# A DLRM tower on one core: gathers and gram by tiles of 128 samples, vecT held twice, an MLP block in front of each gram, ids 128 rows deep

## The reference

```python
e = jnp.stack([tbl_0[ids[:, 0]], ..., tbl_25[ids[:, 25]]], axis=1)
sd = jnp.einsum('bfd,bd->bf', e, dense)
ss = jnp.einsum('bfd,bgd->bfg', e, e)
pairs = ss[:, iu, ju]                      # triu, k=1
z = jnp.concatenate([dense, sd, pairs], axis=1)
h = jnp.concatenate([z, dense], axis=1)
h = jnp.maximum(h @ W_top1 + b_top1, 0.0)  # 512
h = jnp.maximum(h @ W_top2 + b_top2, 0.0)  # 256
y = h @ W_top3                             # 1
```

## Time and profile before

| | before |
|---|---|
| median of 3 runs | 405.81 us (405.66 to 406.05) |
| profiled execution, its own time | 407.06 us |
| span of the profiled execution, first to last instruction | 405.1 us |
| mean granted TensorE clock | 0.966 of full speed |
| PE busy | 360.1 us, 89% of the span |
| POOL busy | 261.0 us, 64% |
| DVE busy | 232.0 us, 57% |
| ACT busy | 185.9 us, 46% |

### The profile page before, as it was taken

How to read it: one execution, slowest core, us unless ns; L and a number is a source line. 1 busy time by engine, 2 the same in 40 slices (tenths; PEclk the granted TensorE clock), 3 DMA queues, 4 the chain that set the end, 5 groups by cost and what they waited for, 6 DMA issues and landing times.

```text
span 405.1 us, 13256 instructions
## 1 busy us (share of the span) xinstructions
PE 360.1 (89%) x6020; PEld 311.2 (77%) x6020; DVE 232.0 (57%) x326; ACT 185.9 (46%) x266; POOL 261.0 (64%) x279
## 2 busy tenths in 40 slices
PE   1965987968999989998999999998999899998895
PEld 0954976957888978897879878897879888897763
DVE  3999767862556825685557825684557835541300
ACT  2475523742137622674237623674147613673231
POOL 5777777777777777777777777777777777100000
PEclk9996698995999999999999999999999999999999
DMA  7867222222222222222222222222222222100000
GB/s 193 210 165 267 79 55 57 52 54 58 57 67 53 53 55 55 66 57 57 56 67 53 53 55 64 58 57 56 56 67 53 53 55 68 21 2 3 3 0 0
DMA packets 12271, 26.46 MB, mean 65 GB/s; under 512 B 5296, under 2 KB 6448, under 8 KB 12089
## 3 DMA queue, kind: packets, MB, share of 16 engines
q0 software_dynamic: 8704, 17.84, 17.7%
q1 hardware_dynamic: 3513, 7.79, 6.9%
HBM read 25.61 MB, written 0.01 MB: 63 GB/s over the span
## 4 chain that ended last, share of the span: by engine, by line
PE 77%; POOL 8%; issue 5%; ACT 4%; DMA 3%; DVE 2%; DVEq 0%; SPq 0%
PE sum_bank L421 31%; PE vec_bank L447 12%; PE work_bank L472 10%; POOL rows L224 8%; PE work_bank L482 7%; PE vec_bank L437 6%; PE work_bank L468 5%; PE id_bank L405 3%; DMA rows<-in_tbl,ids_all 2%; PE work_bank L490 2%; DVE onehot L260 1%; ACT late L350 1%; PE work_bank L460 1%; ACT vecT L325 1%; ACT vecT L318 1%
## 5 line engine op out<-in xcount | busy, mean ns | idle before, releaser
L224 POOL DMA_INDIRECT rows<-in_tbl,ids_all x272 | 260.2, 957 | 84.7 <-issue 79.6
L260 DVE TENSOR_TENSOR onehot<-id_bank,row_f 125x1024 fp32r<-125x1024 f32 x144 | 170.7, 1221 | 44.5 <-PE id_bank L405 27.9
L421 PE MATMUL sum_bank<-onehot,parts 125*128 125x256 f32 x1152 | 179.2, 303 | 6.5 <-DVE onehot L260 4.9
L421 PEld LDWEIGHTS sum_bank<-onehot,parts 125*128 125x128 f32 x1152 | 154.7, 200 | 19.7 <-issue 17.4
L325 ACT COPY vecT<-vec_bank 128x512 f32<-128x512 f32 (+1 forms) x72 | 86.3, 1199 | 13.4 <-PE vec_bank L437 13.4
L271 DVE STREAM_TRANSPOSE late<-late 128x832 f32<-128x832 f32 x16 | 28.8, 1798 | 95.8 <-ACT late L334 95.8
L318 ACT COPY vecT<-sum_bank 128x256 f32<-128x256 f32 x72 | 48.6, 678 | 45.1 <-PE sum_bank L421 44.9
L447 PE MATMUL vec_bank<-vecT 128*26 128x26 f32 x4096 | 53.0, 193 | 14.9 <-ACT vecT L325 9.7
L447 PEld LDWEIGHTS vec_bank<-vecT 128*26 128x26 f32 x4096 | 44.3, 104 | 25.9 <-ACT vecT L318 11.6
L437 PE MATMUL vec_bank<-ident,rows 128*128 128x128 f32 x272 | 44.5, 286 | 12.6 <-DMA rows<-in_tbl,ids_all 12.5
L334 ACT COPY late<-vec_bank 128x416 f32<-128x416 f32 x32 | 16.2, 505 | 77.7 <-PE vec_bank L447 75.4
(11 more groups left out here) (22 smaller groups left out, 73.5 us busy)
## 6 DMA issues: line engine op xcount, KB each, us to landing
rows<-in_tbl,ids_all POOLq DMA_INDIRECT x272, 2.5
late<-in_tbl SPq DMA_DIRECT2D x9, 480.0 KB
w_all<-in_weights SPq DMA_DIRECT2D x1, 1540.0 KB, 9.8
xT<-in_dense_t SPq DMA_DIRECT2D x8, 128.0 KB, 2.6
late<-in_weights SPq DMA_DIRECT2D x1, 256.0 KB, 2.7
ids_all<-in_ids SPq DMA_DIRECT2D x1, 208.0 KB, 2.5
late<-in_tbl SPq DMA_DIRECT2D x9, 20.0 KB
vecT<-in_ids_t SPq DMA_DIRECT2D x1, 72.0 KB
```

Of the source, the lines that this page charges most:

```text
L224: nc.gpsimd.indirect_dma_start(rows[:, j, n, t, :], None, tables[f], bass.IndirectOffsetOnAxis(ids_all[:, TD * d + t, f:f + 1], 0)).then_i ...
L260: nc.vector.tensor_tensor(onehot[:, use % RING, 0:width, :], bass.AP(got.tensor, got.offset, [got.ap[0], [0, width], [1, DS]]), bass.AP(nu ...
L421: last = nc.tensor.matmul(sum_bank[into % 2][:, 0:DS], parts[:, part, CH_AT[n] + c0 + c, :], onehot[:, use % RING, c, :], start=(p % PER = ...
```

## The change

What it does, part by part:

- The 17 gathered features go by tiles: the gathers of a tile (17) are issued before those of the next, `transpose_rows` takes four features of one tile (groups of 4, 4, 4, 4 and 1, so 5 groups for a tile), and their places in `vecT` follow in a row. There are still 272 gathers, and buffers for two tiles of them.
- `vecT` is held twice (one for each parity of the step), so that the next step's vectors can be written before this step's grams are done.
- Gram goes by tiles: two calls (h = 0, 1) for each tile, and the rest of the work on TensorE is cut in two halves, one for each tile: 9 packs of step d+1, the groups of the next tile, the pairs of this one.
- A unit of the MLP stands between a tile's last transposes and the next tile's first gram: `layer2(d-1, 0)` after tile 2d, `layer1(d, 0)` after tile 2d+1. The other units are spread behind the grams.
- `idsT` and `pick` are 128 rows deep, where they had 36 (the ids are filled up with rows of zeros); the ids' DMA brings 256 KB for 72 KB.
- The last step's MLP goes by tiles of 128 samples: that of tile 14 stands behind the grams of tile 15.
- `w1x` is summed on VectorE after the first `turn`, no longer at the end of the first step. `dots` is held once.
- The weights' rows are sorted on the host to the new places (`order`, `pair_row`); the amount of arithmetic is the same.

The core of the diff (left out: the same order written once more for ScalarE's drains, the counters, and the host's sorting):

```diff
-    FG = 2
+    FG = 4
...
-    ROWS_AT_FIRST = {1: 0, 3: 1, 5: 2, 7: 3, 9: 4, 11: 5, 13: 6, 15: 7, 17: 8}
-    ROWS_AFTER = {4: 1, 5: 2, 7: 3, 9: 4, 11: 5, 13: 6, 15: 7, 17: 8}
-    TURN_AFTER = {RING - 1: 0, RING + 1: 1}
-    PAIRS_AFTER = {6: 0, 10: 1}
-    X_AFTER = 8
+    ROWS_AT_FIRST = {3: 0, 6: 1, 9: 2, 12: 3, 15: 4}
+    ROWS_AFTER = {2: 0, 4: 1, 5: 2, 7: 3, 8: 4}
+    TURN_AFTER = RING + 1
+    LATE_LAYER1_AFTER = 3
+    PAIRS_AFTER = 6
+    X_AFTER = 7
...
-        vecT = sb("vecT", [P, DS, VECS])
+        vecT = sb("vecT", [P, 2, DS, VECS])
...
-        idsT = sb("idsT", [STEPS * NH // TWO, TWO * DS], fp32r)
+        idsT = sb("idsT", [P, TWO * DS], fp32r)
...
-        pick = sb("pick", [STEPS * NH // TWO, STEPS * NH // TWO], fp32r)
+        pick = sb("pick", [P, SPREADS], fp32r)
...
-            for d in range(STEPS):
+            for tile in range(TILES):
                 for j in range(GROUPS):
-                    if d:
-                        pool.wait_ge(vec_filled, rows_at(d - 1, j) + 1)
+                    if tile >= TD:
+                        pool.wait_ge(vec_filled, rows_at(tile - TD, j) + 1)
                     for n, f in enumerate(group(j)):
-                        for t in range(TD):
-                            nc.gpsimd.indirect_dma_start(
-                                rows[:, j, n, t, :], None, tables[f],
-                                bass.IndirectOffsetOnAxis(ids_all[:, TD * d + t, f:f + 1], 0)
-                            ).then_inc(gathered[j], 16)
+                        nc.gpsimd.indirect_dma_start(
+                            rows[:, tile % TD, FG * j + n, :], None, tables[f],
+                            bass.IndirectOffsetOnAxis(ids_all[:, tile, f:f + 1], 0)
+                        ).then_inc(gathered[tile % TD][j], 16)
...
+            for tile in range(TILES):
+                d, t = tile // TD, tile % TD
+                for k in range(HP):
+                    if d + 1 < STEPS:
+                        set_pack(d + 1, HP * t + k)
+                    if k == TURN_AFTER:
+                        turn(tile)
+                        if tile == 0:
+                            dve.wait_ge(weights_loaded, 16)
+                            dve.wait_ge(w1x2_loaded, 16)
+                            nc.vector.tensor_tensor(w1x, w1x, w1x2, ALU.add).then_inc(w1x_summed, 1)
...
+            for tile in range(TILES - 1):
+                d, t = tile // TD, tile % TD
+                for h in range(2):
+                    gram(tile, h)
+                    if t == 0 and d:
+                        layer1(d - 1, 1 + h)
+                    if t == 1 and d and h == 0:
+                        layer2(d - 1, 1)
+                    if t == 1 and d and h == 1:
+                        layer3(d - 1)
+                    table_step(d + 1, HP * t + h)
+                for k in range(2, HP):
+                    table_step(d + 1, HP * t + k)
+                    if k in ROWS_AFTER:
+                        transpose_rows(tile + 1, ROWS_AFTER[k])
+                    if t == 0 and d and k == LATE_LAYER1_AFTER:
+                        layer1(d - 1, M1 - 1)
+                    if k == PAIRS_AFTER:
+                        transpose_pairs(tile)
+                if t == 0 and d:
+                    layer2(d - 1, 0)
+                if t == 1:
+                    if d == 0:
+                        pe.wait_ge(w1x_summed, 1)
+                    layer1(d, 0)
+                if tile == TILES - 2:
+                    layer2(d - 1, 1)
+                    layer3(d - 1)
...
+            for h in range(2):
+                gram(TILES - 1, h)
+                last1(0, 2 * h)
+                last1(0, 2 * h + 1)
+            last2(0)
+            transpose_pairs(TILES - 1)
+            for m in range(M1):
+                last1(1, m)
+            last2(1)
```

More of the change, by code:

```diff
@@ L13 @@
 KT, KP = 3, 126
+GATHERED = [f for f in range(FEATS) if f not in ONEHOT]
 TILES = 16
@@ L152, in build @@
         weights_loaded, w1x2_loaded = sem("weights_loaded"), sem("w1x2_loaded")
-        gathered = [sem(f"gathered{n}") for n in range(GROUPS)]
+        gathered = [[sem(f"gathered{t}_{n}") for n in range(GROUPS)] for t in range(TD)]
         ident_zero, ident_set, pick_set = sem("ident_zero"), sem("ident_set"), sem("pick_set")
@@ L316, in drain_sum @@
                 use = NH * d + n
+                if n == 0 and d >= 2:
+                    act.wait_ge(vec_filled, gram_at(TD * (d - 2) + TD - 1, 1) + 1)
                 act.wait_ge(pack_done, PER * use + PER)
[L318 to L323, removed]
+                nc.scalar.copy(vecT[:, d % 2, :, place(ONEHOT[n] + 1)], sum_bank[use % 2][:, 0:DS]
+                               ).then_inc(sum_drained, 1)
@@ L460, in transpose_pairs, with unit1 @@
                     last = nc.tensor.transpose(work_bank[use % 2][0:KP, b * P:(b + 1) * P],
-                                               pairs[:, t, b * KP:(b + 1) * KP], ident[:])
+                                               pairs[:, tile % TD, b * KP:(b + 1) * KP], ident[:])
+                last.then_inc(work_filled, 1)
+            def unit1(use, d, m, s0, ns):
+                free_work(use)
+                cols, out = slice(m * P, (m + 1) * P), work_bank[use % 2][:, 0:ns]
+                nc.tensor.matmul(out, w1x[:, cols], xT[:, d % 2, s0:s0 + ns], start=True, stop=False)
+                if m == 0:
+                    pe.wait_ge(work_drained, use)
+                for b in range(KT):
+                    last = nc.tensor.matmul(out, w1p[:, b, cols], pairsT[0:KP, b, s0:s0 + ns],
+                                            start=False, stop=(b == KT - 1))
+                last.then_inc(work_filled, 1)
@@ new lines, in unit2, with unit3 @@
+            def unit2(use, m, s0, ns):
+                free_work(use)
+                if m == 0:
+                    pe.wait_ge(work_drained, use)
+                for b in range(M1):
+                    last = nc.tensor.matmul(work_bank[use % 2][:, 0:ns], w2_sb[:, b, m * P:(m + 1) * P],
+                                            h1[:, b, s0:s0 + ns], start=(b == 0), stop=(b == M1 - 1))
+                last.then_inc(work_filled, 1)
+            def unit3(use, s0, ns):
+                pe.wait_ge(work_drained, use)
+                for b in range(M2):
+                    last = nc.tensor.matmul(work_bank[use % 2][0:1, 0:ns], w3_sb[:, b:b + 1], h2[:, b, s0:s0 + ns],
+                                            start=(b == 0), stop=(b == M2 - 1))
@@ L474, in layer1 @@
-                last.then_inc(work_filled, 1)
-            def layer2(d, m):
-                use = NW * d + W2 + m
-                free_work(use)
-                if m == 0:
-                    pe.wait_ge(work_drained, NW * d + W2)
-                for b in range(M1):
-                    last = nc.tensor.matmul(work_bank[use % 2][:, 0:DS], w2_sb[:, b, m * P:(m + 1) * P],
-                                            h1[:, b, :], start=(b == 0), stop=(b == M1 - 1))
-                last.then_inc(work_filled, 1)
@@ L486, in layer3 @@
-            def layer3(d):
-                use = NW * d + W3
-                pe.wait_ge(work_drained, use)
-                for b in range(M2):
-                    last = nc.tensor.matmul(work_bank[use % 2][0:1, 0:DS], w3_sb[:, b:b + 1], h2[:, b, :],
-                                            start=(b == 0), stop=(b == M2 - 1))
-                last.then_inc(work_filled, 1)
+                unit1(layer1_at(d, m), d, m, 0, DS)
+            def layer2(d, m):
+                unit2(layer2_at(d, m), m, 0, DS)
```

317 lines of the change are left out of this document (165 added, 152 removed).

## The result

The changed kernel takes 378.16 us in the median (377.58 to 379.46) where the kernel before takes 405.74 beside it: the ratio is 0.932, with a 95% interval of 0.929 to 0.936. The profiled execution took 377.58 us, its span is 375.8. Run again later, beside two other kernels, it took 378.31 us.

A forecast was written before the change was run, and what follows sets the result against it. PE was taken as the bound at 44.93 us a step, with POOL's gathers next at 42.5. Tile 15's gram at 353.1 plus 3 for clock and 22 for tail gave a 378.1 us span, 378.8 median; range 374 to 388.

The forecast's parts named there:

- main case: Whole kernel: PE's steps become shorter than POOL's, so the last gathers bound the end; 378.8 us median, chance 0.60.
- Start: Up to the first gram: it starts at 47.1 us against 53.06, with 0.7 added for the larger ids' DMA.
- Tiles 0 and 1: From the first gram to the gram of tile 2: 31.95 us, which puts the latter at 79.05.
- Step: PE's full step: 44.93 us falls to 43.3 without the waits, then to 41.55 with ids 128 rows deep.
- the filled hole: In front of the gram in each step: a 1.73 us unit of the MLP fills a 1.4 us hole.
- POOL: Tile 15: PE waits for the last gathers, the last starting at 345.39; first gram of tile 15 at 353.1 us.
- Clock: Around the gram of tile 15: half clock after PE's waits costs 3 us (0 to 5).
- Tail: From the first gram of tile 15 to the end of the span: 22 us.
- From span to median: Whole execution: span 378.1 us, 1.96 outside it, profiled execution 1.25 above the median, so 378.8 as median.
- the depth is worth nothing: Rival on the 128-row ids: no gain, PE keeps 43.3 us a step; median 381.6 us, chance 0.20.
- ScalarE comes late: Rival in front of each gram: 14 tiles still wait 1.2 us each; about 390 us, chance 0.13.
- The issue stops: Rival behind each of 30 grams from tile 1: PE stands 1.66 us for instructions; about 424 us, chance 0.03.

## Why the prediction was right

The time was 378.16 for 378.8 predicted, and the main case is what happened: PE's steps become shorter than POOL's, and the last gathers bound the end. That the number is this close is in part luck, as the last point shows. By its steps:

- *Start.* 47.69 for 47.1. The first split began at 8.11 instead of 7.12, 1.0 later and not 0.7, and the run with 36 rows gives 1.2 at the gram. But the runs don't tie this to the bytes of the ids' DMA: with 72 rows (144 KB) the split began at 8.16 too, and in the run with gathers by step, at 128 rows, at 6.76.
- *Tiles 0 and 1.* 34.2 us for 31.95 (the terms as written give 31.92), the term of the sum that was furthest off. The gram of tile 1 has no unit in front of it, which the diff shows and I missed (1.28), and two grams had issue stops of 0.54 and 0.40. So the gram of tile 14 came at 330.65 for 328.4. This did not reach the end, because there PE waits for POOL.
- *Step.* 41.46 for 41.55. Here two terms are separated by runs: the spreading (0.37 measured, 0.39 counted), and the filled hole, whose 1.4 us was right for the kernel before; without the unit the changed kernel would wait 0.95 for each of 14 tiles. The spreading's gain lies in other places than counted. The transposes in front give the 0.18, but from the spreading's start to the next lookup it takes 0.24 to 0.44 us in the 22 spreadings from 115 us on (0.24 in four of them), where 0.23 was expected, and the lookup behind gives the rest. All else in the step, four grams, two layers and a layer 3 in other places with the hole, gives 1.67 against the kernel before with 128 rows, where 1.6 was counted.
- *POOL.* The last gather starts at 345.19 for 345.39; the waits for rows at the end are where they were expected. That they cost 6 us, clock included, is shown by the run without tile 15's gathers.
- *Clock.* Half clock from about 344 to 351 cost 1.5 in layer 2, not 3: it ended earlier than after 90.73, and a part of it fell on the stop itself. The gram of tile 15 came at 354.2, for 356.1 with the 3 us in it.
- *Tail.* 21.6 for 22; the 128-column instructions take 0.11 as the transposes did.
- *From span to median.* The span was 375.8 for 378.1, 2.3 less than counted; but the median lies 2.4 above the span and not 0.7, as the profiled execution was 0.6 below the median this time. The two errors nearly cancel, and the hit is closer than the working.

Of the rivals, "the depth is worth nothing" is refuted by two runs, although the rule of the Trainium skill ("TensorE: Matmul & The Clock Gate", section "LDWEIGHTS (loading the stationary operand)") that a load's time goes by its columns is not: the load itself takes 0.19 us at 128 rows and 0.18 at 36. What differs is whether it runs beside its neighbours. "ScalarE comes late" did not happen: between 79 and 330 us PE has no wait that the profile shows. The issue stops exist, at 0.2 to 1.3 us in the kernels with the new order, and only where little stands between two grams of a tile; in the steady steps of the changed kernel there is none.

The value of the order by tiles was right in sum but not understood: the run with gathers by step shows a ring of waits between PE and POOL that I had not worked out.

## What to carry to other kernels

Before an edit on the busiest engine is priced, find the next pace that cannot be made faster: here 272 gathers at 1.25 us each, on an engine shown as 69% busy, took a saving of 11.2 us at the gram of tile 14 down to 4.6 in the time. Where that second queue ends, put work that does not need its last result, and check that this work is not itself behind a copy in another engine's queue. When two engines hand buffers to each other in a fixed order, write down which buffer each transfer waits for; the order of issue alone moved this kernel by 72 us.

## What the runs showed of the hardware

- A matmul of 36 rows between matmuls of 125 to 128 rows costs 0.37 us more than one of 72 or 128 rows. No weight load overlaps on either side of it. Filling the operands up with zero rows is worth it: 10.6 us in the kernel before, for 36 such matmuls.
- The granted clock fell to half some 1.7 us into a stop of PE of 3.92 us, and in another run 0.5 us behind a stop of 1.91 us; with stops of 0.4 to 0.6 us, and one of 1.33 inside a gram, it stayed at full. What PE did before differs between them, so this is no rule.
- A gram call is 128 matmuls and 128 weight loads in under 2 us. In the kernels with the new order the second of a tile's two calls lost 1.00 to 1.33 us to "issue" with one short unit (8 matmuls of 128 columns) between them, in three runs; at most 0.36 with two short ones or one of 256 columns; up to 0.91 with one pack (tiles 0 and 1); and none with a unit and a pack. The cause was not tried.
